# Spectral block and gated scan: spectra kept on chip, column transforms in tiles of 64 rows, a weight ring of two

## What is computed

```python
# layer 0
xn = layernorm(x); xf = rfft2(xn, axes=(1, 2), norm="ortho")       # 32 x 17 frequencies
o1 = einsum("bhwni,hwnio->bhwno", xf.reshape(B, 32, 17, 8, 24), w1c) + b1c   # own 24x24 blocks per frequency
o1 = complex(relu(o1.real), relu(o1.imag))
xs = irfft2(o1, s=(32, 32), norm="ortho")
x = xs + x + mlp(layernorm(xs))                                      # 192 -> 768 -> 192, gelu
# layer 1
u = xn @ Wu + bu;  g = sigmoid(xn @ Wg + bg)                         # xn = layernorm(x)
h = 8 steps of  h = g * (h @ A) + (1 - g) * u
x = x + h;  x = x + mlp(layernorm(x))
```

## Time and profile before

| | us |
|---|---|
| median of three runs | 1189.8 |
| all three | 1189.80, 1190.35, 1184.14 |
| profiled execution | 1189.59 |
| its span | 1187.8 |
| TensorE busy | 1072.2 (90% of the span) |
| VectorE busy | 805.0 (68%) |
| ScalarE busy | 725.3 (61%) |
| GpSimd busy | 352.5 (30%) |
| mean granted TensorE clock | 0.954 |

### The profile page before, as it was taken

One profiled execution on the slowest core, in us unless ns is written; L12 is line 12 of the kernel. 1 busy time (PEld: TensorE's weight loads), 2 busy tenths in 40 slices (PEclk: granted clock), 3 DMA queues, 4 the chain that ended last, 5 costly groups with the idle time before them and its releaser, 6 DMA issues. The chain is left out here.

```text
span 1187.8 us, 25740 instructions
## 1 busy us (share of the span) xinstructions
PE 1072.2 (90%) x9160; PEld 822.2 (69%) x9160; DVE 805.0 (68%) x2102; ACT 725.3 (61%) x1325; POOL 352.5 (30%) x384
## 2 busy tenths in 40 slices
PE   2659999994899999999799999999999599999998
PEld 1239888882487888888555655655654388888887
DVE  4826555641768886776768689699699657666665
ACT  2646565651766667666677566567535266766665
POOL 1260011211322222221238437348257211111110
PEclk9869999996899999999899999999999699999999
DMA  6978799896300000000100000000000000000001
GB/s 131 291 176 159 153 183 183 169 194 149 100 6 1 0 0 0 0 0 0 47 1 2 1 1 1 1 1 1 1 1 1 1 14 26 27 27 26 26 26 40
DMA packets 140217, 64.21 MB, mean 54 GB/s; under 512 B 115824, under 2 KB 134928, under 8 KB 140128
## 3 DMA queue, kind: packets, MB, share of 16 engines
q1 hardware_dynamic: 132888, 37.42, 15.6%
q0 software_dynamic: 5600, 18.76, 5.9%
q10 hardware_dynamic: 1648, 6.91, 1.8%
HBM read 44.21 MB, written 12.58 MB: 48 GB/s over the span
## 5 line engine op out<-in xcount | busy, mean ns | idle before, releaser
L1092 PE MATMUL L_conv_ps<-w2hl,L_conv_hhi 128*128 128x384 f32 x768 | 228.2, 365 | 8.1 <-DVE X L992 7.5
L908 ACT ACTIVATE L_conv_hf<-L_conv_ps,L_conv_b 128x512 f32<-128x512 f32 x192 | 132.1, 688 | 150.9 <-PE L_conv_ps L1073 142.3
L982 DVE TENSOR_TENSOR L_conv_hlo<-L_conv_hf,L_conv_hhi 128x512 fp32r<-128x512 f32 x192 | 139.8, 742 | 104.0 <-ACT L_conv_hhi L917 101.7
L1092 PE MATMUL L_conv_ps<-w2hl,L_conv_hlo 128*128 128x192 f32 x768 | 188.3, 252 | 0.0
L861 POOL TENSOR_TENSOR X<-X,L_conv_b 128x192 f32 x128 | 72.5, 598 | 358.2 <-DVE L_conv_xn L967 358.2
L1207 POOL TENSOR_TENSOR sc_lo<-XS,sc_hi 128x512 fp32r<-128x512 f32 x96 | 142.4, 1499 | 114.2 <-ACT sc_hi L1283 114.2
L1092 PEld LDWEIGHTS L_conv_ps<-w2hl,L_conv_hhi 128*128 128x128 f32 x768 | 144.2, 188 | 14.7 <-DVE L_conv_hlo L982 7.2
L1092 PEld LDWEIGHTS L_conv_ps<-w2hl,L_conv_hlo 128*128 128x128 f32 x768 | 146.1, 191 | 0.0
L638 PE MATMUL psF<-spectrum,X 100*24 100x64 f32 x4352 | 128.7, 290 | 13.2 <-issue 10.3
L1283 ACT ACTIVATE sc_hi<-XS 128x512 fp32r<-128x512 f32 x144 | 87.6, 629 | 81.9 <-DVE XS L1348 27.6
L638 PEld LDWEIGHTS psF<-spectrum,X 100*24 100x24 f32 x4352 | 121.3, 122 | 23.0 <-issue 22.6
(11 more groups left out here) (150 smaller groups left out, 2141.7 us busy)
## 6 DMA issues: line engine op xcount, KB each, us to landing
X<-in_L_conv_w SPq DMA_DIRECT2D x136, 144.0 KB
XS<-in_x POOLq DMA_DIRECT2D x8, 768.0 KB, 6.8
rows_spectrum<-XS POOLq DMA_DIRECT2D x8, 768.0 KB, 4.6
d<-rows_spectrum ACTq DMA_DIRECT2D x8, 768.0 KB, 5.0
X<-in_x SPq DMA_DIRECT2D x8, 768.0 KB, 8.5
out<-X SPq DMA_DIRECT2D x15, 384.0 KB, 2.6
XS<-d POOLq DMA_DIRECT2D x59, 96.0 KB, 4.8
spectrum<-in_L_conv_mlp_w SPq DMA_DIRECT2D x2, 576.0 KB, 9.5
```

Of the source, the lines that this page charges most:

```text
L908: nc.scalar.activation(hf[:, m % 3, :], ps[:, RB + m % 2, :], gelu, bias=b1[:, m:m + 1]).then_inc(act1, 1)
L982: nc.vector.tensor_tensor(hlo[:, m, :], hf[:, m % 3, :], hhi[:, m, :].bitcast(F32), ALU.subtract).then_inc(h_lo, 1)
L1092: mm = pe.matmul(o, x, w, start=(m == 0 and n == 0), stop=(m == MT - 1 and n == 1), skip_group_check=True)
```

## The change

- The spectra stay on chip. `X` becomes the eight groups `d2[g]`, all present at once. After row step k SyncE moves `d1` there in one SBUF to SBUF transfer (`gather`, 128 rows of 6 KB); `rows_spectrum` and `spectrum_rows` are gone. The inverse writes its result over the group (`d3[g]` is `d2[g]`).
- The 128 partitions of a group are laid out anew: real and imaginary parts of one frequency on 64 partitions, the other frequency on the other 64. The column transform is then a matmul of 64 rows and 64 columns per frequency, two for each image, where it was one of 128 by 128. The inverse becomes four matmuls of 64 by 64 per half, copied out by two instructions on each engine. The Nyquist unit, and group 0's inverse, keep whole columns.
- VectorE spreads the first frequency and ScalarE the second, where each had four of eight images; the Nyquist unit takes 12 spreads on each engine, before 24 of half the size.
- The weight ring has two places in memory of their own. SyncE's pieces are issued two at a time, four times a unit, the biases last.
- `scatter` is one transfer of 768 KB per group, issued by SyncE between the weights: after the first two pieces of unit `last_of[g] + 5` for groups 0 to 4, at the end for groups 5 to 7, and the MLP weights behind those. GpSimd no longer takes part.
- All eight slabs of `X` are loaded in `inverse_rows`, after all scatters.

```diff
-RING = 4
+RING = 2
...
+        d2 = [X[:, B * g:B * (g + 1), :] for g in range(NG)]
+        d3 = [d2[g].rearrange("p b c -> p (b c)") for g in range(NG)]
+        Wt = [sb(f"W{r}", [P, 2, H, BS, 2])[0:HALF + NH] for r in range(RING)]
...
+        def gather(eng, k):
+            eng.dma_start(X[k:P:TPB, :, :].rearrange("p (g b) c -> p g (b c)", g=NG),
+                          d1[k % 2].rearrange("p b c -> p (b c)")).then_inc(d2_in[k % 2], 16)
+        def scatter(eng, g):
+            eng.dma_start(XS[g:P:NG, :, :].rearrange("p (t b) c -> p t (b c)", t=TPB), d3[g]).then_inc(sh.rows_in, 16)
...
+            for k in range(TPB):
+                sp.wait_ge(d1_done, 4 * (k + 1))
+                gather(sp, k)
+                if k >= TPB - PIECES:
+                    load_piece(0, k - (TPB - PIECES))
+            for i in range(PIECES):
                 load_piece(1, i)
             for u in range(2, UNITS):
+                for i in range(PIECES):
+                    sp.wait_ge(mixed, STEP * (u - 2) + STEP // PIECES * (i + 1))
                     load_piece(u, i)
+                    for g in range(NG):
+                        if (u, i) == (last_of[g] + 5, 0):
+                            sp.wait_ge(d3_v, copies(g, 1))
+                            sp.wait_ge(d3_a, copies(g, 1))
+                            scatter(sp, g)
...
         # TensorE, columns(u)
-                for b in range(B):
-                    bank, col = at + b // 4, P * (b % 4)
-                        mm = pe.matmul(ps[0:HALF, bank, col:col + P], d2[g % 2][:, b, HALF * s:HALF * (s + 1)],
-                                       fwd_h0[:, 0:P] if g == 0 else fwd_h[:, :], start=True, stop=True)
+                for b, k in itertools.product(range(B), range(2)):
+                    out = ps[0:HALF, col_bank(u) + k, 2 * H * b:2 * H * (b + 1)]
+                        table, s, rows = fwd_h0 if g == 0 else fwd_h, units[u][1], (lower, upper)[k]
+                        mm = pe.matmul(out, d2[g][rows, b, HALF * s:HALF * (s + 1)], table[rows, 0:2 * H],
+                                       start=True, stop=True)
...
         # TensorE, inverse(g, half)
+                if g or half:
+                    before = copies(g, half - 1) if half else copies(g - 1, 1)
+                    pe.wait_ge(d3_v, before)
+                    pe.wait_ge(d3_a, before)
+                if g:
+                    for j, k in itertools.product(range(2), range(2)):
+                        rows, cols = (lower, upper)[k], (lower, upper)[j]
+                        at = 4 * NH * (2 * half + j)
+                        pe.matmul(ps[cols, 6 + k, 0:NH * HALF], inv_h[rows, 0:2 * H], z[rows, at:at + 4 * NH],
+                                  start=True, stop=True, skip_group_check=True).then_inc(inv_done, 1)
```

More of the change, by code:

```diff
@@ L69, in dft_tables @@
     z = np.zeros((2 * H, 2 * H))
[L70 to L84, removed]
+    real = fc.copy()
+    real[H:] = 0
+    nyquist = np.zeros((2 * H, 2 * H))
+    nyquist[H:] = fc[0:H]
+    fwd_h = np.concatenate([fc[spread], fc[spread]])
+    fwd_h0 = np.concatenate([np.concatenate([real[spread], fc[spread]]), np.concatenate([nyquist[spread], z])], 1)
+    ib = ic[halves][:, spread]
+    real, last = ic.copy(), np.zeros((2 * H, 2 * H))
+    real[:, H:] = 0
+    last[:, H:] = ic[:, 0:H]
+    real, last = real[halves][:, spread], last[halves][:, spread]
+    first = np.block([[real, z], [z, ib]])
+    inv_h = np.concatenate([np.concatenate([ib, ib]), first, np.block([[last, z], [z, z]]), np.block([[z, z], [last, z]])], 1)
+    return [np.ascontiguousarray(a.astype(np.float32)) for a in (fwd_w, inv_w, fwd_h, fwd_h0, inv_h)]
 def block_ones():
@@ L336, in load_piece @@
             def load_piece(u, i):
[L337 to L342, removed]
@@ L364, in _ @@
+            for g in range(NG):
+                if last_of[g] + 5 >= UNITS:
+                    sp.wait_ge(d3_v, copies(g, 1))
+                    sp.wait_ge(d3_a, copies(g, 1))
+                    scatter(sp, g)
+            for dst, src in sh.mlp_loads("L0_conv_"):
                 sp.dma_start(dst, src).then_inc(sh.raw_in, 16)
[L365 to L368, removed]
         @block.gpsimd
@@ L379, in _ @@
                 load(k)
[L380 to L384, removed]
-            n_vectors = sh.load_vectors(pool)
[L388 to L392, removed]
+            for k in range(XT, TPB):
+                load(k)
+            n_vectors = sh.load_vectors(pool)
             pool.wait_ge(sh.vectors_in, 16 * n_vectors)
@@ new lines, in inverse @@
+                for j in (2 * half, 2 * half + 1):
+                    out = ps[:, 6 + j % 2, 0:NH * HALF]
+                    pe.matmul(out, inv_h[:, 2 * H:2 * H + P], z[:, 4 * NH * j:4 * NH * (j + 1)], start=True, stop=False,
+                              skip_group_check=True)
+                    for s in range(2):
+                        at = 2 * H + P * (s + 1)
+                        mm = pe.matmul(out.rearrange("p (b s c) -> p b s c", b=2, s=2)[:, :, s], inv_h[:, at:at + P],
+                                       Zn[:, 2 * j:2 * j + 2, :, 0:BS], start=False, stop=True, skip_group_check=True)
+                    mm.then_inc(inv_done, 2)
```

178 lines of the change are left out of this document (62 added, 116 removed).

## The result

The changed kernel takes 1208.6 us (1207.96 to 1209.76, four runs) against 1188.6 (1184.14 to 1190.35, four runs): a ratio of 1.0175, 95% interval 1.0145 to 1.0206. Its profiled span is 1206.6 us. Forecast were 1161.8.

The account below looks back on a forecast made before the run. TensorE's own work was taken to set the Fourier stage, with DMA close behind. Savings of 6.2 + 0.6 + 5.3 + 5.9 + 5.4 + 4.4 = 27.8 us from 1189.6 gave 1161.8 us, range 1148 to 1182.

Parts of the forecast that it names:

- the rest products: Middle: what a unit on TensorE holds besides column and inverse transforms; no change to it was forecast.
- (a): Rival, middle: tiles of 64 run one after another, columns +13.2, inverse +15.3, kernel 1201.5 us; chance 0.08.
- Step 1: Start: spectra kept on chip, transfer taken as 4.6 us, columns at 71.0 instead of 77.25, 6.2 us less.
- Rival (d): Start and end: the transfer on chip is slow, 8.5 us, +4 at each, kernel 1170 us; chance 0.09.
- Steps 2 and 3: Middle: paired column tiles 1.6 us (5.3 less, plus 0.6 ahead of the loop), quadrant inverse 0.85 us (5.9 less).
- Step 4: Middle: scatter by SyncE between the weights costs nothing, with 3 us of margin; units fall from 10.95 to 10.0 us.
- rival b: Middle: weights come late, the loop's 11.2 us are eaten by waits, kernel 1173 us; chance 0.17.
- Step 5: End of the loop: with X's reload moved out, TensorE's stop in the last unit is gone, 5.4 us less.
- Step 6: Tail: row transforms start 14 us behind the products' end, against 18.35, 4.4 us less.
- Step 7: Behind the last scatter: loading all eight slabs of X there costs nothing, nearly 20 us cover a delay.
- rival c: Row transforms and MLP entry: the 5.44 us stop moves there under X's loads, kernel 1167 us; chance 0.12.

Follow-up runs that it names:

- e1: Kernel before with only the products' h order of the change (moving spectra 4 bytes apart, weights 192): 1212.9 us, ratio 1.0237.
- e2: Changed kernel with forward table columns permuted so the moving spectra of even and odd h lie 64 bytes apart: 1189.8 us, ratio 1.0024 to the kernel before.
- c1: e2 with the gathers issued by GpSimd on the x loads' queue instead of by SyncE: 1188.3 us, ratio 1.0051 to the kernel before.
- p1: e2 with the gather sent to partitions 4 apart in each half of 64 instead of 8 apart, in two transfers: 1190.1 us, ratio 1.0021.
- c2: c1 with gather and scatter sent to partitions at stride 4 in halves of 64: 1178.8 us, ratio 0.9957 to the kernel before.
- f2: c2 with whole scatters at stride 8 as in the changed kernel, the last one in two parts of four images: 1176.5 us, ratio 0.9921.
- c3: c2 with the scatters on GpSimd's queue too: 1180.0 us, ratio 0.9965 to the kernel before.
- f1: c2 with the last scatter in two parts of four images, the first issued after the first half of the inverse: 1179.7 us, ratio 0.9940.
- f3: f1 with the first unit's weights released after the last row step: 1183.2 us, ratio 0.9968 to the kernel before.
- g1: f2 with each of the five scatters beside the products cut into four, one part behind each weight piece: 1175.3 us, ratio 0.9913.
- g2: f2 with all eight scatters after the last weights: 1177.8 us in one run.
- e4: Changed kernel with permuted tables, moving spectra of even and odd h 32 bytes apart: 1186.4 us in one run.
- e6: Changed kernel with permuted tables, moving spectra of even and odd h 16 bytes apart: 1185.6 us in one run.
- w0: e2 with the weights of the first two units loaded only, reused by all later units: 1168.4 us in one run.
- p2: p1 with the scatter's destination partitions at stride 4 as well: 1187.8 us, ratio 1.0006 to the kernel before.
- e5: Kernel before with the early reload of four slabs of X left to the row transforms: 1182.2 us, ratio 0.9962.
- e3: Changed kernel with weights of even and odd h 3072 bytes apart, moving spectra still 4 bytes apart: 1212.1 us in one run.

## Why the prediction was wrong

Forecast and median are 46.8 us apart. By its steps:

- **The step that failed is one that is missing**: "the rest products" were a constant. The diff changed their h order, and with it the distance of two moving operands from 64 to 4 bytes. It costs 17 x 2.17 = 36.9 us of products. That the order is the cause is shown from both sides: e1 put it in, e2 took its effect out. The whole kernel moved by less, 28 and 19 us. In the changed kernel 7 us came back: TensorE idled 0.4 us in the middle instead of 4.5, at a clock of 0.99 instead of 0.97. That its lower DMA share (0.72 for 0.89) is the reason is argued, not shown. No rival had this step; (a) came near the result, 1201.5, for a reason that is refuted.
- **Step 1** (start, -6.2): +9.9. The nearest row, the write of 4.6 us, was of the wrong kind: a gather lands after 10.9 us and takes more engine time than the write, and the x loads, which the row steps wait for, land after 12.0 instead of 6.8. Neither the queue alone (c1, x loads 12.5) nor the placement alone (p1, 11.7) mends that, both do (c2 8.8, f2 7.9). Even then the columns start at 76 to 82 us (c2, c3, f1 to f3, g1, g2), not at 71. The step is unsteady: e2, e4, e6 and w0 have one and the same start and begin their columns anywhere from 82 to 93. Rival (d), 8.5 us, thought of the landing alone.
- **Steps 2 and 3** (tiles of 64): right, 1.58 and 0.81 us against 1.6 and 0.85. A unit of e1, with the old forms and the slow products, takes 12.8 us (185.7 to 198.5), the changed kernel's 11.8.
- **Step 4** (scatter, nothing; rival b): no weight came late in the changed kernel. Once the products are fast again, scatters and weights together do cost 12 us (g2 against f2), as stops on TensorE and a clock at 1.2 GHz, not as the waits of (b). The waits of (b) do come up in three versions whose scatters SyncE issues in halves: in all 2.8 us in p2, 3.7 in c2, 1.7 in f1. That the slow products gave the DMA engines slack, which hid all this in the changed kernel, is argued.
- **Step 5** (stop, -5.4): right. e5 alone gives 0.0038 x 1184.5 = 4.5 us, and g2 brings the stop back with other transfers. What TensorE lacks in such a stop is open. Its instructions are a candidate, since the page lists instruction queues among those of the 16 DMA engines (q8, 0.93 MB), but no run shows it.
- **Step 6** (tail, -4.4): -2.8. The last copy ends 9.2 us behind the products, not 8, and the row transforms begin 6.3 us behind it, not 5 (the scatter lands after 6.1 us by the page, not 4.6). The prediction's own 8 and 5 make 13, where it wrote 14.
- **Step 7** (X, nothing; rival c): right. From the first row transform to the first sum with X it is 48.8 us (312.24 to 361.00), before 48.5, so nothing stopped there.

The misses, span against span: start 9.9 + 6.2 = 16.1; middle 13.0 + 16.6 = 29.6, the products' 36.9 less the 7.3 that came back; tail 4.4 - 2.8 = 1.6; the first columns and everything behind the row transforms -0.7; in all 46.6.

## What to carry to other kernels

Read a diff for what it does to the addresses of an operation that it leaves alone: an index order that looks free sets how far apart concurrent tiles read. Keep the moving operands of tiles that run at once 16 bytes or more apart, the least distance that was free here. Put a transfer that nobody waits for behind the one that is waited for, on the same queue, and spread its destination partitions; here only both together paid. When TensorE stands still and waits for no engine, look at the DMA share in the stop and just before it, and at the clock of the microseconds behind it.

## What the runs showed of the hardware

- Four f32 column tiles at once, neighbours in pairs reading moving operands 4 bytes apart: 337 ns a matmul, against 290 at 16, 32 and 64 bytes. Stationary operands 192 bytes apart cost nothing against 3072 (e3 against the changed kernel, and e2).
- Beside such matmuls ScalarE's relu of 512 columns took up to 2181 ns instead of 1102 (e2). At 16 and 32 bytes it still took up to 1447, with the matmuls at their 290: there ScalarE is slowed and TensorE is not.
- Behind stops of 1.41 and 0.50 us that no engine released, TensorE's granted clock was 0.50 and the columns took 2.83 us instead of 1.57 (f2).
- A transfer of 768 KB from SBUF to SBUF landed after 10.9 (changed kernel) and 12.0 us (e2) beside x loads, and after 6.1 in the place of the scatter.
